# Score matmuls on 32-row tiles of dense keys, and value products of two key chunks at a time

## What is computed

```python
sim = jnp.einsum('bhid,bhjd->bhij', q, k) * scale
a = jax.nn.softmax(sim, axis=-1)
out = jnp.einsum('bhij,bhjd->bhid', a, v)
...
x = _attn(h1, h1, q1, k1, v1, o1_w, o1_b, heads) + x
h2 = _ln(x, n2_g, n2_b)
x = _attn(h2, context, q2, k2, v2, o2_w, o2_b, heads) + x
h3 = _ln(x, n3_g, n3_b)
proj = h3 @ ff_w1 + ff_b1
a, g = jnp.split(proj, 2, axis=-1)
ff = a * jax.nn.gelu(g, approximate=False) @ ff_w2 + ff_b2
```

## Time and profile before

| | us |
|---|---|
| median of 3 runs (lowest to highest) | 1166.69 (1151.57 to 1182.37) |
| profiled execution, span | 1156.2 |
| PE busy | 1111.4 (96%), 7808 records |
| weight loads busy | 709.2 (61%) |
| DVE busy, ACT busy | 692.4 and 690.1 (60% each) |
| POOL busy | 74.1 (6%) |
| DMA queue of the program | 13.1% of 16 engines, 31000 packets |
| PE's share of the chain that ended last | 88% |

### The profile page before, as it was taken

How to read it: one execution, slowest core, us unless ns; L and a number is a source line. 1 busy time by engine, 2 the same in 40 slices (tenths; PEclk the granted TensorE clock), 3 DMA queues, 4 the chain that set the end, 5 groups by cost and what they waited for, 6 DMA issues and landing times.

```text
span 1156.2 us, 21296 instructions
## 1 busy us (share of the span) xinstructions
PE 1111.4 (96%) x7808; PEld 709.2 (61%) x7808; DVE 692.4 (60%) x1607; ACT 690.1 (60%) x1440; POOL 74.1 (6%) x129
## 2 busy tenths in 40 slices
PE   8999999999999999999999999999999999999979
PEld 5556566666565566666656556666666656666544
DVE  3877567746446567764737765775553556677510
ACT  4557666766564565766655666676565456666630
POOL 3000000000001100000000000000000110000000
PEclk9999999999999999999999999999899899999975
DMA  6110011100130001101131001110022100101000
GB/s 188 44 33 19 11 33 38 29 19 23 34 105 20 24 24 38 28 20 29 25 93 29 19 15 30 31 38 19 10 46 80 44 20 23 42 20 31 7 6 6
DMA packets 31101, 40.24 MB, mean 35 GB/s; under 512 B 10388, under 2 KB 22296, under 8 KB 30360
## 3 DMA queue, kind: packets, MB, share of 16 engines
q1 hardware_dynamic: 31000, 38.89, 13.1%
HBM read 10.97 MB, written 0.66 MB: 10 GB/s over the span
## 4 chain that ended last, share of the span: by engine, by line
PE 88%; ACT 4%; DVE 4%; issue 2%; DMA 0%; POOLq 0%; POOL 0%; DVEq 0%; ACTq 0%
PE st_ps L779 17%; PE pv_ps L835 16%; PE mx_ps L798 16%; PE sp_ps L762 10%; PE sp_ps L761 9%; PE sp_ps L880 4%; PE sp_ps L995 2%; PE sp_ps L812 2%; PE sp_ps L862 2%; DVE mx L1228 2%; PE sp_ps L954 2%; PE sp_ps L942 2%; ACT probs L1067 1%; ACT oT L1074 1%; PE sp_ps L897 1%
## 5 line engine op out<-in xcount | busy, mean ns | idle before, releaser
L1228 DVE TENSOR_REDUCE mx<-mx_ps 128x1 f32<-128x512 f32 (+2 forms) x720 | 475.7, 686 | 201.6 <-PE mx_ps L798 198.4
L1067 ACT ACTIVATE probs<-st_ps 128x512 f32<-128x512 f32 x720 | 400.6, 597 | 193.6 <-PE st_ps L779 187.1
L798 PE MATMUL mx_ps<-ring,qT 128*128 128x512 f32 (+2 forms) x864 | 293.4, 398 | 4.6 <-DVE mx L1228 2.0
L779 PE MATMUL st_ps<-qT,ring 128*128 128x256 f32 (+1 forms) x1408 | 275.8, 298 | 4.9 <-ACT probs L1067 2.8
L779 PEld LDWEIGHTS st_ps<-qT,ring 128*128 128x128 f32 (+1 forms) x1408 | 217.6, 189 | 80.2 <-ACT probs L1067 41.9
L835 PE MATMUL pv_ps<-probs,v 128*9 128x256 f32 (+3 forms) x2944 | 223.8, 377 | 3.0 <-ACT probs L1067 2.3
L798 PEld LDWEIGHTS mx_ps<-ring,qT 128*128 128x128 f32 x864 | 142.2, 190 | 91.4 <-DVE mx L1228 45.4
L835 PEld LDWEIGHTS pv_ps<-probs,v 128*9 128x9 f32 (+2 forms) x2944 | 44.8, 90 | 64.2 <-issue 18.8
L1116 ACT ACTIVATE kdense<-sp_ps 128x512 f32<-128x512 f32 (+2 forms) x116 | 57.4, 539 | 36.0 <-PE sp_ps L880 34.1
L1311 DVE SCALAR_TENSOR_TENSOR gate<-sp_ps,cols,gate 128x256 f32<-128x256 f32 x40 | 17.9, 480 | 76.4 <-ACT gate L1174 41.1
L1054 ACT ACTIVATE ks<-sp_ps 128x320 fp32r<-128x320 f32 x80 | 35.2, 441 | 47.3 <-PE sp_ps L862 28.7
(11 more groups left out here) (142 smaller groups left out, 1067.3 us busy)
## 6 DMA issues: line engine op xcount, KB each, us to landing
ring<-kdense SPq DMA_DIRECT2D x256, 64.0 KB, 2.0
wb<-in_w_blk SPq DMA_DIRECT2D x4, 1520.0 KB, 7.0
ring<-kdense SPq DMA_DIRECT2D x160, 32.0 KB, 1.8
ring<-kdense SPq DMA_DIRECT2D x32, 127.0 KB, 2.3
wb<-in_w_blk SPq DMA_DIRECT2D x4, 280.0 KB, 7.5
ring<-oT SPq DMA_DIRECT2D x16, 64.0 KB, 2.0
ctx_n<-in_ctx SPq DMA_DIRECT2D x4, 192.0 KB, 6.2
x<-in_x SPq DMA_DIRECT2D x4, 160.0 KB, 3.4
```

The lines of the kernel that those rows point to most:

```text
L779: mm = pe.matmul(st_ps[s % N_ST][0:kr, i * a["nq"]:(i + 1) * a["nq"]], key_op(n, h)[:, c * P:c * P + kr], query_op(u, b)[:, h // of(u), :] ...
L798: mm = pe.matmul(mx_ps[o % N_MX][0:rows, j * a["nk"]:(j + 1) * a["nk"]], query_op(u, b)[:, h // of(u), tt * P:tt * P + rows], key_op(n, h) ...
L1067: nc.scalar.activation(probs[0:kr, s % N_P, 0:w], st_ps[s % N_ST][0:kr, 0:w], ACT.Exp, scale=float(a["dh"]) ** -0.5).then_inc(S["probs_rea ...
L1228: nc.vector.tensor_reduce(mx[b][0:rows, t, heads[0]:heads[-1] + 1], mx_ps[(o - 1) % N_MX][0:rows, 0:a["hpm"] * a["nk"]].rearrange("p (h k) ...
```

## The change

The padded ring, its DMAs (464 of them), its clearing and its zeroing at the start are gone. `rows_of` names the 32 (or 64) partitions of a head, and both operands of a score matmul are cut to these rows, so that the matmul uses a row tile of the array: rows 0, 32, 64 or 96, all 128 columns. The keys come from `kdense` itself, now stored as fp32r, and for u 4 from a new buffer `kca`.

A `st` slot now holds one head and two key chunks, where it held two heads and one chunk. Both of its matmuls are thus on the same rows of the array, and the next slot is the next head's. A `pv` step takes two key chunks, eight matmuls, where it took four; `probs` has twelve places for six. In self attention a `max` step holds both query tiles of one head. The number of matmuls of each kind is as before: 1472 of scores by keys, 896 for the maxima, 1472 of `pv`.

```diff
-N_P = 6
-RING = 4
...
+N_P = 12
...
+def max_items(u, qd):
+
+    hs = range(4 * qd, 4 * qd + 4)
+    if u == 4:
+        return [([TQ], ATT[u]["nq"], [h, h + 2]) for h in hs[:2]]
+    if ATT[u]["nk"] == SQ:
+        return [(list(range(TQ)), P, [h]) for h in hs]
+    return [([t], P, [h]) for t in range(TQ) for h in hs]
+
+
+def score_slots(u, qd):
+
+    hs = range(4 * qd, 4 * qd + 4)
+    if u == 4:
+        return [[(0, [(h + k, c) for k in (0, 2) for c in range(2)]) for h in hs[:2]]]
+    return [[(k, [(h, c) for c in (2 * k, 2 * k + 1)]) for h in hs] for k in range(-(-ATT[u]["nk"] // SQ))]
...
+        kca = two("kca", [P, 4, SQ], FR)
...
-        ring = sb("ring", [P, RING, 4, SK], FR)
...
+        def rows_of(u, h):
+
+            j, sr = h % of(u), ATT[u]["sr"]
+            return slice(j * sr, (j + 1) * sr)
...
-                nc.vector.memset(ring[:, :, :, :].bitcast(F32), 0.0)
...
-                            sp.dma_start(ring[rows, n % RING, region(u, h), 0:a["nk"]].bitcast(F32),
-                                         dense_keys(u, b, g)[rows, 0:a["nk"]]).then_inc(ring_in[n % RING], 16)
...
-                        for i, h in enumerate(sl["heads"]):
+                        for i, (h, c) in enumerate(sl["cells"]):
+                            kr, g, rs = chunk_rows(a["nk"], c), h // of(u), rows_of(u, h)
                             mm = pe.matmul(st_ps[s % N_ST][0:kr, i * a["nq"]:(i + 1) * a["nq"]],
-                                           key_op(n, h)[:, c * P:c * P + kr], query_op(u, b)[:, h // of(u), :],
+                                           key_op(u, b)[rs, g, c * P:c * P + kr], query_op(u, b)[rs, g, :],
                                            start=True, stop=True)
                         mm.then_inc(S["scores_full"], 1)
...
-                        for j, h in enumerate(heads):
+                        for j, (h, t) in enumerate((h, t) for h in heads for t in ts):
+                            g, rs, tt = h // of(u), rows_of(u, h), 0 if t == TQ else t
                             mm = pe.matmul(mx_ps[o % N_MX][0:rows, j * a["nk"]:(j + 1) * a["nk"]],
-                                           query_op(u, b)[:, h // of(u), tt * P:tt * P + rows],
-                                           key_op(n, h)[:, 0:a["nk"]], start=True, stop=True)
+                                           query_op(u, b)[rs, g, tt * P:tt * P + rows],
+                                           key_op(u, b)[rs, g, 0:a["nk"]], start=True, stop=True)
...
-                        kr = chunk_rows(a["nk"], c)
-                        for s in mine:
-                            for i, h in enumerate(slots[s]["heads"]):
-                                j = h % 4
-                                v = v20[b][0:kr, c, h, :] if a["dh"] == 8 else v8[b][0:kr, c + (4 if u == 4 else 0), h, :]
-                                mm = pe.matmul(pv_ps[32 * j:32 * j + a["dh"] + 1, 0:a["nq"]], v,
-                                               probs[0:kr, s % N_P, i * a["nq"]:(i + 1) * a["nq"]],
-                                               start=(c == 0), stop=(c == -(-a["nk"] // P) - 1), tile_position=(0, 32 * j))
-                            if s == mine[-1] and c == -(-a["nk"] // P) - 1:
-                                mm.then_inc(S["out_full"], 1)
-                            else:
-                                mm.then_inc(s_used, 1)
+                        cells = sorted((c, h, s, i) for s in mine for i, (h, c) in enumerate(slots[s]["cells"]))
+                        for c, h, s, i in cells:
+                            j, kr = h % 4, chunk_rows(a["nk"], c)
+                            v = v20[b][0:kr, c, h, :] if a["dh"] == 8 else v8[b][0:kr, c + (4 if u == 4 else 0), h, :]
+                            mm = pe.matmul(pv_ps[32 * j:32 * j + a["dh"] + 1, 0:a["nq"]], v,
+                                           probs[0:kr, s % N_P, i * a["nq"]:(i + 1) * a["nq"]],
+                                           start=(c == 0), stop=(c == -(-a["nk"] // P) - 1), tile_position=(0, 32 * j))
+                        mm.then_inc(S["out_full"] if k == quads[n]["n_k"] - 1 else s_used, 1)
...
-                        nc.gpsimd.memset(ring[:, n % RING, :, :].bitcast(F32), 0.0).then_inc(S["cleared"], 1)
```

More of the change, by code:

```diff
@@ L68 @@
 N_MX = 2
-N_P = 6
-RING = 4
+N_P = 12
 PV_LAG = 2
 FIRST_W = 3
-K_LEAD = 4
 TAIL = 40
@@ L196, in plan @@
         put(hi + MTR_DUE, 3, ("mtr", n))
[L197 to L199 removed]
+        for k in range(q["n_k"]):
+            last = max(s for s in q["slots"] if slots[s]["k"] == k)
+            put(last + PV_LAG, 2, ("pv", n, k))
         put(q["slots"][-1] + PV_LAG, 3, ("oev", n))
@@ L786, in _ @@
                         a = ATT[u]
-                        t, rows, heads = quads[n]["items"][i]
+                        ts, rows, heads = quads[n]["items"][i]
                         if i == 0:
-                            last = [s for s in order if s[0] == "q_tr" and s[1] == u and s[2] == b][-1]
-                            taken(pe, last)
-                            pe.wait_ge(ring_in[n % RING], 16 * ring_dmas[n])
+                            for what in ("q_tr", "k_tr"):
+                                taken(pe, [s for s in order if s[0] == what and s[1] == u and s[2] == b][-1])
                         o = value["max_full", step] - 1
```

156 lines of the change are left out of this document (55 added, 101 removed).

## The result

The changed kernel takes 1607.34 us, the median of four executions (1588.06 to 1619.72); the kernel before, beside it on the same chip, takes 1171.21 (1151.57 to 1182.37). The ratio is 1.375, with a 95% interval from 1.350 to 1.401. The forecast was 1560 us, by a clock that falls for long stretches.

A forecast was written before the change was run, and what follows sets the result against it. PE's queue was taken as the bound. 1156 - 57 + 100 - 65 = 1134 us with the clock as it was; half of 1064 us of PE work at 1.2 GHz, 0.8 more each, gave 1560, range 1347 to 1772.

The forecast's parts named there:

- The likeliest case: PE's clock falls to 1.2 GHz for long stretches: 1560 us, 1347 to 1772, chance 0.55.
- Term 1: Value products: 361 stretches become 184, each one saved worth 0.32 us, 57 us less.
- Term 2: Score matmuls on row tiles among full-height work: 501 added changes of form at 0.20 us, 100 us more.
- Term 3: Score matmuls of a quad's heads overlap on four row groups: 65 us less, at most 129, at least nothing.
- Term 4: Dropping the ring's DMAs, clearing and zeroing: nothing, or up to 10 us if a phase's first quad starts sooner.
- Term 5: DVE, the next engine: its reductions and copies keep a bare quad from falling much under 6.3 us.
- The sum at full clock: Whole kernel with the clock as it was: 1134 us, bounds 1010 and 1199.
- The price of 1.2 GHz: PE's matmuls at the lower clock take 1.8 times as long as at 2.4 GHz.
- The share at 1.2 GHz: Half of PE's 1064 us of work runs at the lower clock, from a quarter to three quarters.
- How the clock comes back: After an early fall, mostly behind runs of L995, of which there are eight, mostly over 100 us apart.
- The test that I named for the first cross attention: Clock staying at 1.00 between 40 and 110 us would refute the forecast and leave 1134 us.

The follow-up runs named there:

- full_rows: The changed kernel with every score matmul reading all 128 rows instead of a row tile; 1156.45 us, 0.993 times the kernel before.
- the bench: A separate program of back-to-back matmuls without the attention; 256 columns on 32 rows took 0.12 us on one tile, 0.031 going round four.
- twice_pv: The changed kernel with every value product issued twice into the same sum; 1499.65 us, 1.291 times the kernel before.
- pad_before: The kernel before with the second matmul of every `two_part` product zero-padded from 32 to 128 rows; 1083.55 us, 0.933 times the kernel before.
- one_tile: The changed kernel with all heads of a group reading the first head's rows, so on one row tile; 1860.16 us, 1.600 times the kernel before.
- rows64: The changed kernel with each score matmul reading 64 rows instead of 32; 1472.90 us, 1.253 times the kernel before.
- pad_after: The changed kernel with the second matmul of every `two_part` product zero-padded to 128 rows; 1342.76 us, 1.158 times the kernel before.

## Why the prediction was right, and where it wasn't

The likeliest case came about, 1607 against 1560 with a range from 1347 to 1772. Its mechanism held: full_rows shows that the row tiles of the score matmuls are the cause, rows and changes of form together; the bench shows that 32 rows on one tile let the clock fall with PE busy throughout and without any change of form; and twice_pv that more work on 128 rows makes the kernel faster with as many changes. The near agreement of the numbers, though, is partly luck: errors stood against each other in the sum at full clock, and again in the share and the price of the lower level. By step:

- **Term 1, `pv`, -57 us: too large.** The sixteen take 0.98 us as forecast, but full_rows, which has this and nothing on row tiles, is 8 us faster and not 57, and its bare quad is no shorter at all (7.41 us). The step that failed is to take start-to-start prices for PE's own work, and what PE saves for what the kernel saves: PE waits for the reductions and the exponentials instead.
- **Term 2, changes of form, 0.20 us each: right.** The bench has 0.19; pad_before has 78 us for 376, which is 0.21, with some of it from the clock.
- **Term 3, overlap, 65 of at most 129 us: too small.** By the estimate from one_tile it is 84 to 112. The reasoning for the bound failed too, that two matmuls on the same rows must follow each other so that five steps remain of eight: the bench does just this order in 3.9 times less. The kernel's overlap stayed inside the bound all the same.
- **Term 4, the ring's DMAs and zeroing, nothing.** full_rows, without them, has 8 us for them and the pairing together.
- **Term 5, DVE's floor of 6.3 us in a quad:** near. At full clock a quad repeats after 6.7 us, with waits for DVE and for ACT.
- **The sum at full clock, 1134 us:** the estimate from the trace after is 1118, and the terms as measured give about the same: 1135 for the kernel before at full clock, less 8, plus 100, less the 84 to 112 of the overlap. Term 1 was too large and term 3 too small, and that cancelled. With 1.8 as the price of the lower level it would be 1040.
- **The price of 1.2 GHz, 1.8: too large for the kernel.** PE's own work has 1.86 for a `pv` and 1.64 for the bench's turns between forms (0.51 to 0.31), and the waits for the other engines in a quad don't grow with it; by the executions it is 1.62.
- **The share at 1.2 GHz, half of PE's work: too small.** 79% of the time at 1.62 times the price is 0.485/(0.485 + 0.214), 69% of the work. Less price on more of the work came out near the forecast.
- **How the clock comes back:** wrong in the part that it was mostly behind L995; two of the four returns in the kernel before already came without it. It returned 31 times, seven of them with L956, and a `pv` of sixteen was in front of most others. But it didn't hold: from 780 to 784, just behind the stretch shown above, it was at 0.65 again, so the share came out higher all the same.

The test that I named for the first cross attention, 1.00 or not between 40 and 110 us, came out against 1.00: 0.50 from 40 to 60.

Not settled: how much of the fall is from few rows in the score matmuls and how much from the gaps that changes of form leave inside PE. rows64 changed the rows alone, pad_after rows and changes of form together, and each raised the clock (0.747, 0.722); neither brought it to 1.00.

## What to carry to other kernels

A matmul on 32 rows of one tile takes as long as one on 128 (0.12 us for 256 columns in the bench), and where PE did much of it on one tile, or in turn with 128-row work, its clock halved although the profile shows it busy: read the granted clock beside the busy share, and look at what an edit does to the rows that PE fills. Row tiles pay where long runs of them stand together on all four tiles (3.9 times in the bench); scattered among full-height work they pay 0.2 us at each change of form, here 100 us for 501 added changes against the 84 to 112 us that the overlap gave. Start-to-start prices from a loop with other engines in it hold waits: check them on matmuls alone. A short second product of a split contraction is best padded to the full 128 rows with zeros, which on the kernel before gave 6.7%, more than anything else tried.

## What the runs showed of the hardware that was not expected

- In the bench, eight 256-column matmuls on four row tiles, two on each in a row, run 3.9 times as fast as on one tile at full clock, their weight loads included (0.031 us against 0.12).
- PE at 22.00 of 22.00 us busy with 32-row matmuls on one tile was granted 0.50; at 19.20 of 19.20 with 64-row ones, 1.00.
- 128 and 96 rows in turn cost nothing (0.12 us each), 128 and 32 rows 0.19 us at each turn.
- More work made a kernel faster: 158 us more of value products, about 100 us less time (twice_pv).
- An edit that touches no matmul can lower the clock: with one place less in the ring the executions had 0.934 to 0.962, the kernel before beside them 0.962 to 0.978. By the estimate that is about half of the 4.4% that it costs in time.
- Time at 1.2 GHz costs a whole kernel less than a matmul: 1.58 for a quad with DVE and ACT in it, 1.86 for its value products.
